# Six PSUM banks shared out anew between two streams of an attention kernel: four and two in place of three and three

## The reference

```
h = layernorm(x) * (1 + ca) + sa
q, k, v = split(h @ Wqkv.T + bqkv);  q, k = rope(q), rope(k)
att = softmax(where(causal, q @ k.T / sqrt(32), -inf))
x = x + ga * ((att @ v) @ Wo.T + bo)
...
```

## Time and profile before

| | |
|---|---|
| median of 3 runs | 4920.65 us (4919.97 to 4927.16) |
| the profiled execution | 4923.3 us |
| its span, first to last instruction | 4921.5 us |
| mean granted TensorE clock over the span | 0.93 of full speed |
| PE busy | 4400.7 us, 89% |
| DVE busy | 2712.7 us, 55% |
| ACT busy | 2240.2 us, 46% |
| POOL busy | 1632.7 us, 33% |

### The profile page before, as it was taken

The page is one execution under the profiler, slowest core; times in us unless marked ns, Lnnn a source line. Parts: engine busy times, 40 slices in busy tenths (PEclk is TensorE's granted clock), DMA queues, the critical chain, the costliest instruction groups (busy, mean ns, idle before and its releaser), DMA issues.

```text
span 4921.5 us, 75676 instructions
## 1 busy us (share of the span) xinstructions
PE 4400.7 (89%) x19552; PEld 2341.7 (48%) x19552; DVE 2712.7 (55%) x5795; ACT 2240.2 (46%) x4226; POOL 1632.7 (33%) x1079
## 2 busy tenths in 40 slices
PE   4899999985899999885999999875999999877998
PEld 2445454344445444353445444353545444356776
DVE  2546556564546546474555646464554646475565
ACT  1356556721355657521355657531465657421111
POOL 1142534311142534312152434302153443303554
PEclk7899999986899999997899999987899999978999
DMA  3111112122111112122112112122121212128998
GB/s 126 44 35 49 49 44 61 57 87 78 48 38 49 50 33 70 48 93 78 41 40 50 49 31 70 58 92 73 37 57 36 54 34 72 59 79 222 257 258 199
DMA packets 185430, 369.47 MB, mean 75 GB/s; under 512 B 44340, under 2 KB 47540, under 8 KB 183348
## 3 DMA queue, kind: packets, MB, share of 16 engines
q1 hardware_dynamic: 163512, 306.26, 21.9%
q0 software_dynamic: 21504, 58.40, 5.1%
HBM read 195.48 MB, written 84.68 MB: 57 GB/s over the span
## 4 chain that ended last, share of the span: by engine, by line
PE 75%; issue 11%; DVE 5%; ACT 4%; DMA 2%; POOL 1%; POOLq 1%; ACTq 1%; SPq 0%; DVEq 0%
PE PS L1070 22%; PE PS L1032 14%; PE PS L1052 10%; PE PS L1015 9%; PE PS L1172 5%; PE PS L1023 5%; PE PS L1183 3%; PE PS L1098 2%; ACT Pt L901 2%; PE PS L1055 1%; DMA xin<-x 1%; PE PS L1111 1%; DVE stA L1252 1%; PE PS L1158 1%; PE PS L1143 1%
## 5 line engine op out<-in xcount | busy, mean ns | idle before, releaser
L901 ACT ACTIVATE Pt<-PS 128x512 f32<-128x512 f32 (+3 forms) x2560 | 1230.2, 534 | 936.5 <-PE PS L1055 476.8
L1316 DVE TENSOR_REDUCE part<-PS 128x1 f32<-128x512 f32 x1536 | 1021.3, 686 | 968.4 <-PE PS L1032 966.0
L1070 PE MATMUL PS<-Pt,V 128*64 128x512 f32 (+3 forms) x5120 | 1280.3, 561 | 0.0
L1052 PE MATMUL PS<-QK 97*128 97x512 f32 (+3 forms) x2560 | 880.1, 409 | 62.4 <-ACT Pt L901 43.0
L1032 PE MATMUL PS<-QK 96*128 96x512 f32 (+3 forms) x2560 | 891.3, 431 | 32.1 <-DVE part L1316 17.8
L791 POOL TENSOR_TENSOR ot<-ot,od 32x512 f32<-32x512 f32 x256 | 325.6, 1272 | 1626.5 <-ACT od L887 1620.8
L1032 PEld LDWEIGHTS PS<-QK 96*128 96x128 f32 x2560 | 403.3, 195 | 876.3 <-DVE part L1312 350.1
L1312 DVE CUSTOM_DVE_ANT_0 PS<-PS,consts 128x384 f32<-128x384 f32 (+3 forms) x1024 | 500.8, 495 | 244.1 <-PE PS L1032 242.4
L1052 PEld LDWEIGHTS PS<-QK 97*128 97x128 f32 x2560 | 482.1, 194 | 248.5 <-ACT Pt L901 102.4
L1015 PE MATMUL PS<-hT,W 128*128 128x512 f32 x1024 | 465.8, 600 | 14.0 <-ACTq L528 14.0
L1070 PEld LDWEIGHTS PS<-Pt,V 128*64 128x64 f32 x5120 | 256.1, 135 | 311.5 <-issue 249.9
(11 more groups left out here) (152 smaller groups left out, 4273.5 us busy)
## 6 DMA issues: line engine op xcount, KB each, us to landing
QK<-st SPq DMA_DIRECT2D x768, 128.0 KB, 2.4
Wg<-wgu SPq DMA_DIRECT2D x48, 768.0 KB
Wd<-wdn SPq DMA_DIRECT2D x48, 384.0 KB
xin<-x SPq DMA_DIRECT2D x16, 1024.0 KB, 6.2
table<-modd SPq DMA_DIRECT2D x64, 256.0 KB, 4.0
xc<-x SPq DMA_DIRECT2D x16, 1024.0 KB, 7.6
out<-x SPq DMA_DIRECT2D x16, 1024.0 KB, 4.3
table<-h SPq DMA_DIRECT2D x16, 1024.0 KB, 6.3
```

The lines of the kernel that those rows point to most:

```text
L901: nc.scalar.activation(Pt[:, t % NPT, first:CH], S2[t % NS2][:, first:CH], ACT.Exp, scale=SCALE).then_inc(exp_done, 1)
L1052: last = mm(S2[t % NS2][:, first:CH], QK[0:3 * HD + 1, hh % 2, 1, k * P:(k + 1) * P], QK[0:3 * HD + 1, hh % 2, 0, j * CH + first:(j + 1) * ...
L1070: last = mm(O[j % 2][2 * i * HD:2 * (i + 1) * HD, first:CH], values_and_ones(g, kb + i, hh % GH), Pt[:, (2 * n + i) % NPT, first:CH], star ...
L1316: v.reduce_max(part[:, qb, cc:cc + 1], s1[:, 0:w], AX.X).then_inc(s1_dve, 1)
```

## The change

S1, the banks for maxima, projections and transposed rows, goes from three to four; S2, the banks for transposed scores, from three to two. Together they are still banks 0 to 5; O keeps 6 and 7. Order, tiles and every instruction are the same; what changes is which bank each writes and which earlier reader PE waits for.

```diff
-NS1 = NS2 = 3
+NS1, NS2 = 4, 2
...
-        S1 = [PS[:, 0], PS[:, 1], PS[:, 2]]
-        S2 = [PS[:, 3], PS[:, 4], PS[:, 5]]
+        S1 = [PS[:, 0], PS[:, 1], PS[:, 2], PS[:, 3]]
+        S2 = [PS[:, 4], PS[:, 5]]
         O = [PS[:, 6], PS[:, 7]]
```

## The result

| | before | after |
|---|---|---|
| median, us | 4919.97 (4918.28 to 4927.16, 5 runs) | 4950.37 (4945.24 to 4952.09, 5 runs) |
| span of the profiled execution | 4921.5 | 4948.6 |
| mean granted clock | 0.934 | 0.936 |

The ratio is 1.0058, 95% interval [1.0044, 1.0073]: slower by 0.6%, where 4953 us had been forecast. (The five runs of before were made on the same chip as those of after; their median is 0.7 us from the one above the prediction.)

The account below looks back on a forecast made before the run. PE in its written order bounds the steady part, a bank mattering only where PE must wait for one; 4923.3 + 42 (scores' third bank) - 10 (fourth bank in the opening) = 4955.3, as median 4953 us; range 4932 to 4988.

Parts of the forecast that it names:

- The loss: Steady part: scores with two banks wait where ACT is late with copies or blocked; 10.6 us a batch, +42 us.
- first, unit 6: Units 4 to 6 of a head: unit 6's second score load 0.18 us late, 12 heads, 2.2 us a batch.
- second, unit 10: Units 9 and 10: score load 0.14 us late in 8 ordinary heads, 0.49 in 4 blocked ones, per batch.
- third, unit 16: Units 15 and 16: second score load 0.37 us late in 9 ordinary heads, 0.49 in 4 others, per batch.
- blocked heads: Heads 2, 6, 10 (ACT also serves projections) and last head 15 (short units): a score load 0.49 us late.
- Delays are taken up inside a place: Where ACT is late, earlier delays are used up at loads already waiting; only the last late load's delay counts.
- rival 1: Delays are not taken up: each place costs its largest lateness, 92 us less 10, median 5003; chance 0.17.
- The 0.05 us hand-over: A score's weight load starts 0.05 us after the exponential that frees its bank ends.
- The gain: Head 0's opening: with a fourth bank PE leaves each of five maxima groups one reading sooner; 2.6 us a batch, -10.
- The vproj left in the range: The vproj put among the first maxima may start 0.4 us sooner; not counted in the sum.
- The row's hold: Steady part: maxima's waits while a row holds its bank until L1331 (22.0 us, 26 times) lie beside value matmuls; zero.
- rival 4: In the last head stalls bring the clock to its lower level, 36.4 us becoming up to 60; +95, 5048; chance 0.03.

Follow-up runs that it names:

- s32: Changed kernel with three banks for S1 instead of four, two for S2, one bank left idle; 4956.3 us, ratio 1.0067 against before.
- hybrid: Four S1 and two S2 banks only in the opening and first six units of head 0, then three and three; 4908.96 us, ratio 0.9974 against before.
- ringopen: One ring of six banks over both streams up to head 0's twelfth score tile, then three and three as before; 4869.66 us, ratio 0.9894.
- spread42: Changed kernel with ACT's copies spread one per unit over four units, inverse and scale steps four units later; 4903.12 us, ratio 0.9961 against before.
- ring5: Both streams share one ring of five banks in PE's order, the sixth bank idle; 4916.61 us, ratio 0.9991 against before.
- ring6: All six banks in one ring over both streams, each use waiting for the use six back; 4838.24 us, ratio 0.9823 against before.
- ring6spread: ring6 with the edit of spread42, ACT's copies spread over four units; 4884.03 us, ratio 0.9917 against before.

## Why the prediction was right

**The bound.** PE in its written order sets the pace: it held. DVE's and ACT's busy times moved by 2.1 us in 2700 and 0.4 in 2240, and the time followed the starts of PE's loads.

**The loss, +42 forecast, +42.1 measured** (41.4 in s32, where it stands alone). The sum is better than its parts:

| place | forecast, 4 batches | measured | why |
|---|---|---|---|
| first, unit 6 | 8.8 | 13.4 | 0.29 a plain head, not 0.18; nothing in heads 1, 5, 9, as forecast |
| second, unit 10 | 12.4 | 13.1 | 0.14 and 0.48, as forecast; heads 1, 5, 9 0.18 |
| third, unit 16 | 21.2 | 15.6 | 0.24 in plain heads, 0.08 in head 12, not 0.37; 0.49 in blocked heads, as forecast |

So two terms were mis-sized by 5 us each, in opposite directions, and cancelled. The lateness of the loads was right: measured from the head's first score, unit 6's second load is 0.17 us later than in before (0.18), and the one of unit 16 is 0.77 - 0.40 = 0.37 later (0.37), where 0.40 is what the loads of unit 14 are late by from the first two places. What was wrong is that a late load makes what follows late by the same. The value loads behind these two, in before and then in after:

```profile
373.36 0.20 PEld L1070 LDWEIGHTS PS<-Pt,V 128*64 128x64 f32 x4 [0.24 <-ACT Pt L901]
...
393.52 0.20 PEld L1070 LDWEIGHTS PS<-Pt,V 128*64 128x64 f32 x4 [0.37 <-ACT Pt L901]
```

```profile
368.96 0.20 PEld L1070 LDWEIGHTS PS<-Pt,V 128*64 128x64 f32 x4 [0.36 <-issue]
...
389.47 0.20 PEld L1070 LDWEIGHTS PS<-Pt,V 128*64 128x64 f32 x4 [0.25 <-issue]
```

Behind a score load that had waited apart from its partner, the values come 0.42 us later (372.94 to 373.36 in before; 389.04 to 389.47 in after). Behind a pair of loads that went together they come 0.56 later (392.96 to 393.52 in before; 368.40 to 368.96 in after). Why was not tried. In the first place the change turns the one into the other and adds 0.14 to the 0.18; in the third it is the other way round, and 0.14 of the 0.37 comes back. With this term the two places would have been forecast at 0.32 and 0.23, and were measured at 0.29 and 0.24. In the second place and the blocked heads the load waits alone in both kernels, and there the forecast of 0.14 and 0.49 holds within 0.02 (0.18 in heads 1, 5 and 9).

**Delays are taken up inside a place.** Right, and it is what rival 1 hung on. Waits for L901 rose by 43.0 - 25.5 = 17.5 us in the first batch while its heads 1 to 15 grew by 10.6: the rest was taken up at a load that had to wait anyway. A plain head grew by 0.65, a blocked one by 1.25, no head by over 1.5.

**The 0.05 us hand-over.** Right to 0.02 at each of the places read.

**The gain, -10 forecast.** Head 0 gave -12.0; against s32 the fourth bank gave -13.4. It is 3.0 a batch in place of 2.6, from 1.7 to 4.0. The size is near, but the prediction reckoned with waits alone, one reading sooner in each of five groups, and left out the clock of the opening. Head 0's granted clock, 0.72, 0.76, 0.77 and 0.76 in the four batches of before, is 0.80 in all four of after. Over its four cases PE is busy for 274.2 us in before and 260.4 in after, while its idle time did not shrink (14.5 and 16.4 us). So the waits may have given the 2.6 us a batch that were reckoned, or less, with the clock giving the rest, and that the sum came out near can be luck. The vproj left in the range came at twice its size: -3.3 ahead of the first scores in four batches, 0.8 and not 0.4 a batch.

**The row's hold, zero.** Right: no head but the one named changed from after to s32 by over 0.1 us, though the waits for L1331 came and went with the fourth bank.

**Sum.** 27.1 us in the spans, where the forecast has 42 - 10 = 32. The profiled execution of before lies 3.3 us above the median of its five runs and that of after at its own, so that the medians are 30.4 apart.

**What was wrong in "what would show it".** The waits of L1052 for L901 were to go from 40 to over 150; they went to 70. No count of loads stands behind that number. The places that lose are 12, 12 and 13 a batch, 37 in all; the list grew by 30, that is by about one wait a place, and some late loads carry no wait in it at all, as those at 368.41 and 376.76. The time of the waits (over 15 us, measured 17.5) was the sounder half of that sign. PE's busy time was to stay as it is; it rose by 18.4 us, because late matmuls are drawn as longer ones.

**The clock.** In the steady part it stays at 1.00 in after, through 70 such waits and the last head, whose growth is 1.18 us where rival 4 wanted 24. In four other kernels it falls in heads with projections (2, 6 and 10 of each batch), for 3 to 10 us at a time. The Trainium skill, TensorE: Matmul & The Clock Gate, section "A second HAM failure mode: psum-queue depth-cycling", holds that PE standing briefly for banks again and again can make the clock swing; the traces of these four agree in that their clock falls beside such idles, and that of after does not. What sets them apart here is not that PE itself stood, for it did so in after too:

| kernel | longest idle of PE in these heads, us | heads of twelve in which the clock fell |
|---|---|---|
| before, hybrid, ringopen | 0.9 | 0 |
| after, s32 | 0.96 to 0.97 | 0 |
| spread42 | 0.94, and 1.05 behind it | 6 |
| ring5 | 1.2 | 3 |
| ring6 | 1.4 | 2 |
| ring6spread | 1.5 | 12 |

Beside the same idle the clock fell in some batches and not in others; what decides was not tried.

## What to carry to other kernels

A bank taken from a stream cost, here, only what PE's start is late by at the few places where the reader is late; work these places out load by load, and of several late loads in one place count the last. For the side that gets the bank, look at the clock of the stage as well as at its waits. Where two streams that one engine writes in a fixed order each have their own few banks, try one ring over both, each use waiting for the one a ring back: here it beat every split that was tried, 4838 us against 4920 (three and three), 4950 (four and two) and 4909 (four and two in the opening alone), and five banks in a ring did what six did in two halves. Before work is moved later to thin it out, look at which bank it still holds.

## What was not expected of the hardware

- The stretch from the last head to the next batch's first projection took 228.0 us in one kernel and 222.7 in another that has the same instructions there, with a granted clock of 0.76 and 0.80 over 978 to 1202 us.
- In the steady part, which has a clock of 1.00 in before and after, it fell to half in heads with projections beside single idle times of PE of 1.05 to 1.53 us (four value matmuls in 1.98 us in place of 1.08), in 23 of the 48 such heads of four kernels. It did not fall in the 60 such heads of the five kernels whose longest idle there is 0.97 us, nor with 70 waits of weight loads of up to 1.3 us. One fall of 6.8 us made a head 3.17 us longer.
